# The second cross attention's projections, one half of the heads at a time

## The reference

```python
q = (x @ Wq.T).reshape(B, N, H, D)     # 64 rows, 16 heads of 32
k = (y @ Wk.T).reshape(B, L, H, D)     # 1601 rows of context
v = (y @ Wv.T).reshape(B, L, H, D)
attn = jnp.einsum('bnhd,blhd->bhnl', q, k)
attn = jax.nn.softmax(SCALE * attn, axis=-1)
out = jnp.einsum('bhnl,blhd->bnhd', attn, v).reshape(B, N, C)
return out @ Wp.T + bp
```

## Time and profile before

| | us |
|---|---|
| median of 3 runs (1308.42 to 1316.43) | 1315.92 |
| the profiled execution | 1308.3 |
| its span | 1306.5 |
| PE busy | 1161.7 (89%) |
| DVE busy | 634.5 (49%) |
| ACT busy | 425.1 (33%) |
| POOL busy | 338.5 (26%) |

### The profile page before, as it was taken

How to read it: one execution, slowest core, us unless ns; L and a number is a source line. 1 busy time by engine, 2 the same in 40 slices (tenths; PEclk the granted TensorE clock), 3 DMA queues, 4 the chain that set the end, 5 groups by cost and what they waited for, 6 DMA issues and landing times.

```text
span 1306.5 us, 34102 instructions
## 1 busy us (share of the span) xinstructions
PE 1161.7 (89%) x15664; PEld 871.6 (67%) x15664; DVE 634.5 (49%) x977; ACT 425.1 (33%) x806; POOL 338.5 (26%) x366
## 2 busy tenths in 40 slices
PE   7788979796999999998999998999998999653986
PEld 3333434395787887886887887887887887442872
DVE  2011278537125455455455455555555544556286
ACT  1010152223325334334334334433433334121332
POOL 0000000113002333332332332233233332358122
PEclk9899989798999999998999998999998999766999
DMA  9999960712011011011011002002001102200000
GB/s 354 378 371 380 351 262 0 258 68 105 17 47 40 19 54 34 18 55 34 19 34 54 19 22 66 18 22 67 18 23 39 45 23 70 103 3 17 1 2 33
DMA packets 38879, 115.67 MB, mean 89 GB/s; under 512 B 2504, under 2 KB 3016, under 8 KB 34640
## 3 DMA queue, kind: packets, MB, share of 16 engines
q1 hardware_dynamic: 38736, 113.50, 24.2%
HBM read 112.44 MB, written 1.05 MB: 87 GB/s over the span
## 4 chain that ended last, share of the span: by engine, by line
PE 76%; DVE 8%; ACT 6%; SPq 5%; DMA 3%; issue 2%; POOL 0%; DVEq 0%; POOLq 0%; ACTq 0%
PE SB L389 46%; PE SC L1099 6%; PE SB L380 5%; PE SB L1129 4%; SPq L546 4%; DMA R<-in_ctx_t 2%; PE SB L925 2%; PE SC L1108 2%; PE SC L1092 1%; DMA R<-in_ctx 1%; DVE LN L746 1%; ACT R L1615 1%; PE SB L993 1%; PE SB L981 1%; PE SC L901 1%
## 5 line engine op out<-in xcount | busy, mean ns | idle before, releaser
L1414 DVE TENSOR_REDUCE LN<-SC 128x64 f32<-128x768 f32 x128 | 116.6, 952 | 156.8 <-PE SC L1099 156.8
L1615 ACT COPY R<-SB 64x512 f32<-64x512 f32 (+1 forms) x224 | 116.3, 519 | 208.4 <-PE SB L389 206.7
L389 PE MATMUL SB<-high,whigh 128*128 128x512 f32 (+2 forms) x512 | 180.4, 352 | 1.0 <-ACT Z L402 1.0
L389 PE MATMUL SB<-high,wlow 128*128 128x512 f32 (+2 forms) x512 | 178.8, 349 | 0.0
L389 PE MATMUL SB<-low,whigh 128*128 128x512 f32 (+2 forms) x512 | 177.4, 346 | 0.0
L389 PE MATMUL SB<-wlow,high 128*128 128x512 f32 (+1 forms) x416 | 169.8, 408 | 0.0
L389 PE MATMUL SB<-whigh,low 128*128 128x512 f32 (+1 forms) x416 | 166.7, 401 | 0.0
L389 PE MATMUL SB<-whigh,high 128*128 128x512 f32 (+1 forms) x416 | 166.5, 400 | 0.0
L686 POOL TENSOR_TENSOR added<-Z 128x768 f32<-128x768 f32 x32 | 58.7, 1834 | 303.7 <-ACT Z L1647 303.7
L686 POOL TENSOR_TENSOR added<-LN 128x768 f32<-128x768 f32 x32 | 58.4, 1825 | 280.0 <-ACT LN L1647 280.0
L1642 ACT COPY LN<-SC 128x128 f32<-128x128 f32 x64 | 17.0, 265 | 291.1 <-PE SC L1108 290.7
(11 more groups left out here) (224 smaller groups left out, 1878.6 us busy)
## 6 DMA issues: line engine op xcount, KB each, us to landing
R<-in_ctx_t SPq DMA_DIRECT2D x32, 1024.0 KB, 8.1
R<-in_ctx SPq DMA_DIRECT2D x8, 3072.0 KB
R<-in_ctx_t SPq DMA_DIRECT2D x16, 644.0 KB, 7.1
R<-in_f SPq DMA_DIRECT2D x4, 2048.0 KB, 15.4
R<-in_f SPq DMA_DIRECT2D x1, 8192.0 KB, 24.9
R<-in_ctx_t SPq DMA_DIRECT2D x12, 512.0 KB, 3.6
R<-in_Wk SPq DMA_DIRECT2D x3, 1024.0 KB, 11.5
R<-in_Wv SPq DMA_DIRECT2D x3, 1024.0 KB, 13.6
```

The lines of the kernel that those rows point to most:

```text
L389: last = pe.matmul(out_, lhs[a][:, k, :], rhs[b][:, k, :], start=n == 0, stop=n == 3 * NC - 1)
L1414: inc(dve.tensor_reduce(tops[:, r * T:(r + 1) * T], sc_head[:, :, r, 0:6 * T].rearrange("p g (a q) -> p q g a", q=T), AX.XY, ALU.max), "ha ...
L1615: last = act.copy(keys[nu][64 * half:64 * half + 64, pairs, first * P:first * P + full], src[:, :, 0:full])
```

## The change

- `projections(n)` gives the jobs of half batch n (half 0: heads 0 to 7, half 1: heads 8 to 15). A half has 8 key jobs, of one group each, and 7 value jobs. A value job takes up to two tiles, each against 256 of the 512 weight columns, side by side in one bank.
- `FIRST4` projects half batch 0 alone. During batch b the second half of b and the first half of b + 1 are filling; `LAST4` has the second half of the last batch, the output projections with empty places (`-`) between them, and steps `d`.
- There is one region for keys and one for values, so every piece of the context is loaded and split twice per batch. Buffers for pieces are four high and four low instead of two and two; a load waits for the last value job of the piece four before it.
- Scores of pair 0 and pair 4, and the output products of the first and the third group, wait for the copies of their half.
- The queries of the next batch are copied at step `m` of pair 7 and not behind its exponential.
- Weights of the self attention load when the last half is projected; ScalarE makes their high parts behind pairs 5 to 7 (`d`), POOL the low parts and the zeroing in two halves behind pairs 4 to 7 (`prepare5`). `Wp4` loads early. Regions of later stages move. Some semaphores are merged.

```diff
-def projections():
+def projections(n):
-    jobs = []
+    half, jobs = n % 2, []
     for c in range(KC):
-        jobs += [("k", (c, ecs)) for ecs in (((0, 1), (2, 3)) if c == 2 else ((0,), (1,), (2,), (3,)))]
-        if c < KC - 1:
-            jobs.append(("h", c + 1))
-        jobs += [("v", t) for t in piece_tiles(c)]
+        jobs += [("k", (half, c, ec)) for ec in (2 * half, 2 * half + 1)]
+        if KC * n + c + 1 < 2 * KC * B:
+            jobs.append(("h", KC * n + c + 1))
+        t = list(piece_tiles(c))
+        jobs += [("v", (half, c, tuple(t[i:i + 2]) if t[i] + 1 < MF else (t[i],)))
+                 for i in range(0, len(t), 2)]
...
-        for job in jobs[:4]:
+        for job in jobs[:5]:
...
-                each = piece_n(x[0], 1) / 512 * 0.232 if kind == "k" else 0.232
+                each = piece_n(x[1], 1) / 512 * 0.232 if kind == "k" else 0.118
...
-        if pr == HP - 1 and ahead:
-            order.append(("g", 0))
         fill(5.5 if outputs else 4.6, ("e", pr))
+        if ends and pr > 4:
+            order.append(("d", pr - 5))
...
-LATE4 = [("w", t) for t in piece_tiles(KC - 1)]
-EARLY4 = projections()[:-len(LATE4)]
-FIRST4 = [("h", 0), ("q", 0)] + EARLY4[:-2] + [("g", 0)] + EARLY4[-2:]
-BATCH4 = [attention(LATE4 + EARLY4, begins=b == 0, ahead=b < B - 2) for b in range(B - 1)]
-LAST4 = attention(LATE4 + [("y", 0), ("y", 1), ("y", 2)], ahead=False, ends=True)
+FIRST4 = [("h", 0), ("q", 0)] + projections(0)
+BATCH4 = [attention(projections(2 * b + 1) + projections(2 * b + 2), begins=b == 0) for b in range(B - 1)]
+LAST4 = attention(projections(2 * B - 1) + [("-", 0), ("-", 0), ("y", 0), ("-", 0), ("-", 0), ("y", 1), ("-", 0),
+                                            ("-", 0), ("y", 2)], ends=True)
...
+            for i in range(2 * KC * B):
+                if i == 1:
+                    sp.wait_ge(*filled("y3", 3))
+                if i >= BUFS4:
+                    projected(i - BUFS4)
...
+                if i == BUFS4:
+                    inc(sp.dma_start(wp4, natural(Wp4)), "wp4_in", 16)
+            projected(2 * KC * B - 1)
...
+                if n in (0, 3):
+                    inc(pool.memset(qb5[:, n // 3 * B // 2:(n // 3 + 1) * B // 2], 0.0), "zero5")
+                if n:
+                    w = (0, 2, 1)[n - 1]
+                    pool.wait_ge(sem(f"d{w}_split"), 1)
+                    inc(pool.tensor_tensor(dlow[w], dt[w], dhigh[w].bitcast(F32), ALU.subtract), f"d{w}_split")
...
+                        if x in (0, HP // 2):
+                            for n, count in read4("k", 2 * b + (x > 0)).items():
+                                pe.wait_ge(sem(f"read4_{n}"), count)
...
-                        if x == HP - 1 and steps is not LAST4:
-                            queries(b + 1)
+                    elif kind == "m" and x == HP - 1 and steps is not LAST4:
+                        act.wait_ge(sem("s4"), 8 * b + HP)
+                        queries(b + 1)
```

More of the change, by code:

```diff
@@ L188, in at4, with at_half4, read4 @@
     return (AT_LAST4 if steps is LAST4 else AT_BATCH4), b * N_BATCH4 + N_FIRST4
+def at_half4(n):
+    return (FIRST4, 0) if n == 0 else (LAST4 if n == 2 * B - 1 else BATCH4[(n - 1) // 2], (n - 1) // 2)
+def read4(kind, n):
+    at, before = at4(*at_half4(n))
+    jobs = [at[x] for x in at if x[0] == kind and x[1][0] == n % 2]
+    return {bank: before + 2 + max(k for i, k in jobs if i == bank) for bank in {i for i, _ in jobs}}
 def mid_jobs():
@@ L590, in _, with projected @@
             inc(sp.dma_start(bprow, bp4.unsqueeze(0).to_broadcast([P, D])), "bp_in", 16)
[L592 to L620 removed]
+            def projected(i):
+                n, c = i // KC, i % KC
+                at, before = at4(*at_half4(n))
+                bank_, k = max((at[x] for x in at if x[0] == "v" and x[1][:2] == (n % 2, c)), key=lambda a: (a[1], a[0]))
+                sp.wait_ge(sem(f"full4_{bank_}"), before + k + 1)
+            for i in range(2 * KC * B):
[3 more added lines that the diff above has]
+                    projected(i - BUFS4)
+                n, at_ = NC * piece_n(i % KC, 1), NC * piece_keys(i % KC).start
+                inc(sp.dma_start(low[i % BUFS4][:, 0:n], ctxt[i // KC // 2, :, at_:at_ + n]), f"chunk_in{i % BUFS4}", 16)
+                if i == BUFS4:
+                    inc(sp.dma_start(wp4, natural(Wp4)), "wp4_in", 16)
+            projected(2 * KC * B - 1)
             for w, wt in enumerate((Wq5, Wk5, Wv5, Wo5)):
@@ L700, in _ @@
                                            p4_short[w].rearrange("p (r q) -> p r q", q=T), ALU.add), "sums4")
-            at, before = at4(LAST4, B - 1)
-            pool.wait_ge(sem("qb"), B)
-            for late in LATE4[-RING4:]:
-                n, k = at[late]
-                pool.wait_ge(sem(f"full4_{n}"), before + k + 1)
-            inc(pool.memset(qb5, 0.0), "zero5")
-            pool.wait_ge(sem("zero5"), 1)
-            for w in range(3):
-                pool.wait_ge(sem(f"d{w}_in"), 16)
-                split_weight(pool, dt[w], dhigh[w], dlow[w], f"d{w}_split")
+                    if b == B - 1 and pr >= 4:
+                        prepare5(pr - 4)
             pool.wait_ge(sem("pv4"), 4 * B)
@@ L1031, in three_products @@
                 weight = whigh[w][:, :, wcols], wlow[w][:, :, wcols]
-                context = [piece(a[c % 2], c)[:, :, ccols] for a in (high_r, low_r)]
+                context = [piece(a[c % BUFS4], c % KC)[:, :, ccols] for a in (high_r, low_r)]
                 return three_passes(pe, out_, *((weight, context) if keys_first else (context, weight)), within)
-            def keys_read(steps, b, n):
-                done, start = at4(FIRST4, 0) if b == 0 else at4(BATCH4, b - 1)
-                return start + 2 + max(k for (kind, _), (i, k) in done.items() if kind == "k" and i == n)
             def run4(steps, b, u):
                 at, before = at4(steps, b)
-                nxt = 0 if steps is FIRST4 else b + 1
                 def bank4(x):
@@ L1657, in _ @@
             norm_out(act, 4, NT - 1)
[L1660 removed]
+            act.wait_ge(sem("zero5"), 3)
             queries_out(act, "a")
```

240 lines of the change are left out of this document (108 added, 132 removed).

## The result

| | before | after |
|---|---|---|
| median, us (20 runs each) | 1312.1 | 1322.18 |
| ratio to before, 95% interval | | 1.0077 [1.0057, 1.0097] |
| span of the profiled execution | 1306.5 | 1325.4 |
| mean granted clock of TensorE | 0.943 | 0.95 |

The changed kernel is 0.8% slower, outside its own uncertainty and inside the 1% that the prediction called no change. It lies inside the range (1286 to 1328), on the other side of before than the sum of -3.6 us said.

A forecast was written before the change was run, and what follows sets the result against it. TensorE's work and order were taken to bound the kernel, with border waits, the projections before batch 0 and the last batch. Terms -24.1 + 10.5 + 12.1 - 2.1 = -3.6 us gave 1304.7 in the profile, median 1308, range 1286 to 1328.

The forecast's parts named there:

- Term 1: Projections ahead of batch 0's first scores: only half the heads there, 40.2 us instead of 64.35, -24.1 us.
- the walk: Step-by-step timing of engines from a pair's transpose, giving the waits, such as 1.1 and 1.3 us before batch 0.
- Term 2 (a): Seven batches: value tiles as 24 matmuls of 256 columns cost +1.9 us a batch; doubled loading costs nothing.
- the rule: Value projections: columns / 2.4 + 2.5 ns per matmul, making halving cost 3.1 us instead of 15.2; the prediction rejected it.
- Term 2 (b): Batch borders: queries copied sooner, so the 5.3 us lost at each border go.
- (c): Pairs 3 and 7: splits ahead of the maxima copy and subtraction make new TensorE waits, 4.2 us a batch.
- rival B: Batches: the new waits bring the clock down; +13 us at one fall per batch, 1318 in the profile; chance 0.20.
- Term 3: Last batch, now holding half its projections: 98.5 us instead of 86.4, +12.1 us.
- Term 4: Behind the last batch: VectorE's normalised rows wait for less POOL work, -2.1 us.
- A: Batches: the new waits do not come; without any, 36.6 us less, 1268 in the profile; chance 0.24.
- C: Value projections: halved products cost no more than whole ones, 15.2 us less, 1290 in the profile; chance 0.06.
- D: Borders: earlier queries gain nothing because another wait ends last; called the forecast itself; chance 0.50.

The follow-up runs named there:

- q_sooner_fill: Kernel before with queries copied behind pair 7's maxima transpose and six value matmuls moved ahead of a batch's first scores: 1282.82 us, ratio 0.9765.
- deeper: Changed kernel with splits one piece further ahead, at most one behind each pair's `b`, and last-batch loads moved clear of output products: 1271.4 us, ratio 0.9638.
- values_halved: Kernel before with each value tile projected as 24 matmuls of 256 columns instead of 12 of 512: 1328.88 us, ratio 1.0116.
- one_first: Changed kernel looking 7 jobs ahead for splits, none between transpose and `b`, one behind pair 0, weights loaded one per pair: 1276.89 us, ratio 0.9717.
- the second profile: The changed kernel run once more, unedited, for a second profile: ratio to before 1.0075.
- loads_apart: Changed kernel with the four self-attention weights loaded one each behind the scores of pairs 4 to 7 of the last batch: ratio 1.0044.
- splits_ahead: Changed kernel looking 7 jobs ahead instead of 5 for a split of the context: 1293.96 us, ratio 0.9849.

## Why the prediction was right or wrong

- **What bounds the kernel.** Right: TensorE's order, the border's wait for the query copies and the clock behind it. The stall-free 95.35 us was measured by q_sooner_fill as 95.4.
- **Term 1.** Right to 0.1 us: 40.2 forecast, 40.2 measured. deeper, which has neither of its two waits, comes 2.4 us sooner, the 1.1 + 1.3 of the walk.
- **Term 2 (a).** Right: 1.9 a batch forecast, 1.4 by the wait-free periods, 2.0 by values_halved (16 us in 8 batches). The row beat the rule, which the Trainium skill, page "TensorE: Matmul & The Clock Gate", § Back-to-back issue gap, gives for isolated matmuls. Doubled loading cost nothing, as said.
- **Term 2 (b) and (c).** The waits came where they were put. From pair 3's transpose to the end of the subtraction the walk said 7.6 us; the trace has 423.79 to 431.5. On VectorE of the changed kernel, pairs 3 and 4:

```profile
424.10 0.29 DVE L1417 TENSOR_REDUCE mx<-SC 128x1 f32<-128x128 f32 x1 [1.43 <-PE SC L1104]
427.28 2.29 DVE L1392 TENSOR_TENSOR low<-R,high 128x2048 fp32r<-128x2048 f32 x1 [2.89 <-ACT high L1597]
429.49 1.81 DVE L1423 TENSOR_TENSOR LN<-SC,LN 128x768 f32<-128x768 f32 x2
431.22 0.28 DVE L1426 TENSOR_TENSOR LN<-SC,LN 65x128 f32<-65x128 f32 x1
431.42 2.28 DVE L1392 TENSOR_TENSOR low<-R,high 128x2048 fp32r<-128x2048 f32 x1
```

  The low parts stand ahead of the subtraction, and the scores of pair 4 start at 431.64. Against the wait-free pairs of one_first the waits are 1.68 (pair 3), 0.39 (pair 4) and 2.41 (pair 7) = 4.5 us a batch, 4.2 forecast. The price of batch 0's two splits, 2.75, was 2.3 (pair 0: 13.05 against 10.79 with its splits behind `b`).
- **The clock (rival B).** "I take no fall of the clock for these" failed in part. Wait-free 96.8 and waits 4.5 make 101.3, which batch 1 takes; the others take up to 102.7. Per batch that is 0.7 us in this profile and 1.1 in the second, where B put 1.9.
- **Term 3** is the step that failed: 12.1 forecast, 22.6 measured (19.5 in the second profile). The sum of its first part held (scores of pair 0 to those of pair 4: 52.5 against 52.7), in part by luck: the walk put 5.7 us of waits there, most of them for the second split, and the trace has none for a split but a pause of 1.01 us in the first group and 0.69, 1.69 and 1.04 us for VectorE's subtractions and maxima. Its last parts held too (10.2, 8.6 and 14.4 against 10.1, 8.7 and 14.2). Pair 4 was put at 12.8 and took 23.2. The walk counted ScalarE's and VectorE's work beside the output projections, and left out that the four weights load in just that pair. The prediction asked of the context's loads whether they come late, and never of any load what it does to TensorE while it moves. What TensorE waited for was its own next packet of instructions. Against loads_apart the lump costs 8.2 us in the first profile and 5.1 in the second, 3.5 of it in the pause and the rest with the lower clock behind it; 1.5 us are the pause that stays.
- **Term 4.** Right in sign, 0.9 instead of 2.1: one row of VectorE still took 8.0 us (0.55 alone). It begins beside POOL's last subtraction (4.67) and ends with the zeroing behind it (3.50), which both stand behind POOL's last sum. The row of 7.18 us in q_sooner_fill stands beside the same two; that they hold it is read from these times, and no run takes one of them away. VectorE's row, and then POOL's two:

```profile
1207.93 8.02 DVE L749 TENSOR_SCALAR LN<-X,mv,rstd 128x512 f32<-128x512 f32 x1
```

```profile
1207.51 4.67 POOL L689 TENSOR_TENSOR dlow<-R,dhigh 128x2048 fp32r<-128x2048 f32 x1
1212.13 3.50 POOL L716 MEMSET R<- 128x4096 f32 x1
```

- **The rivals.** A (the waits do not come) and C (halved products cost nothing) fell: splits_ahead and values_halved show both prices. B came in part. D, the forecast, had the mechanism: the earlier queries gain nothing in the whole because other waits end last. The sum was short by 14.4 us (-3.6 against +10.8): 10.5 in term 3, 2.7 in term 2, 1.2 in term 4.

## What to carry to other kernels

When an order written by hand feeds several engines, ask of each piece of preparation how many steps of lead it has, not only whether it fits: here the same splits cost 5.2 us a batch ahead of `b` (period 102.0), 5.5 behind it (102.3), and nothing one pair sooner (96.8). Take a change apart before it is judged: its smallest part alone was worth 1.7%, and the rest of it cost that and 0.8% more. And where a bulk load is moved, look at what TensorE issues in those microseconds, not only at who waits for the data: the packets of the instruction queue stand in the trace with their times.

## What was not expected of the hardware

- A pause of TensorE of 5.0 to 5.1 us inside dense small matmuls (a group of 104, 64 columns each) beside 4 MB of loads at 365 GB/s, and of 0.7 to 2.1 us with one load or none. In all twenty cases TensorE goes on 1.3 to 1.5 us after a 16 KB packet of instructions has landed.
- A pause of 0.83 us left the granted clock at 1.00, one of 1.58 us brought it to 0.89 over the next pair, and one of 1.59 left it at 1.00; in the changed kernel waits of 1.9 us did so at some borders and not at others.
- Executions whose program text is the same up to there reach the same instruction up to 9.4 us apart after a third of a millisecond (332.2 to 341.6 in nine profiles; deeper, which splits one piece more ahead of it, has 336.9). That is nearly the 10.1 us by which the medians differ.
